# Attention with two key chunks per value group, transposed sums divided on query partitions, one value buffer and a folded value bias

## What is computed

```
q = layernorm(x) @ Wq.T + bq       # 512 queries per sequence
k = ctx @ Wk.T + bk                # 1601 keys per sequence, from ctx_1024
v = ctx @ Wv.T + bv
16 heads of depth 16
layers 0, 3: attn = softmax(q k^T / 4);  layer 2: attn = sigmoid(q k^T / 4), and no biases
x = x + (attn @ v) @ Wo.T + bo
```

## Time and profile before

| what | value |
|---|---|
| time, median of 3 runs | 3313.81 us (3311.67 to 3315.25) |
| time of the profiled execution | 3315.56 us |
| its span in the profile | 3313.7 us |
| granted PE clock, mean | 0.953 of full |
| PE busy | 2999.2 us, 91% |
| DVE busy | 1761.3 us, 53% |
| ACT busy | 1611.1 us, 49% |
| phase 0 (softmax), about | 0 to 893 us |
| phase 4 (sigmoid), about | 1568 to 2165 us |
| phase 6 (softmax), about | 2369 to 3220 us |

### The profile page before, as it was taken

One profiled execution on the slowest core, in us unless ns is written; L12 is line 12 of the kernel. 1 busy time (PEld: TensorE's weight loads), 2 busy tenths in 40 slices (PEclk: granted clock), 3 DMA queues, 4 the chain that ended last, 5 costly groups with the idle time before them and its releaser, 6 DMA issues.

```text
span 3313.7 us, 42625 instructions
## 1 busy us (share of the span) xinstructions
PE 2999.2 (91%) x16108; PEld 1521.6 (46%) x16108; DVE 1761.3 (53%) x4116; ACT 1611.1 (49%) x2747; POOL 382.8 (12%) x357
## 2 busy tenths in 40 slices
PE   5899999999799889997899999979889999999987
PEld 2234343343377658887332333257533433434333
DVE  3877776778275553332211110046477777777834
ACT  1465665656500112111577777922226656566662
POOL 3000100000110102223100010022301010000000
PEclk7999999999899999998999999989889999999996
DMA  6323224221110001000834432120243233232100
GB/s 159 83 59 77 62 51 89 54 47 24 48 34 26 1 13 45 1 1 20 198 77 105 100 86 61 24 78 1 58 104 64 66 76 62 66 76 47 24 1 30
DMA packets 119187, 190.36 MB, mean 57 GB/s; under 512 B 15900, under 2 KB 82628, under 8 KB 115912
## 3 DMA queue, kind: packets, MB, share of 16 engines
q1 hardware_dynamic: 118984, 187.65, 24.4%
HBM read 133.59 MB, written 53.63 MB: 56 GB/s over the span
## 4 chain that ended last, share of the span: by engine, by line
PE 74%; DVE 11%; ACT 6%; issue 6%; DMA 2%; SPq 1%; POOL 1%; POOLq 0%; ACTq 0%; DVEq 0%
PE psum L189 58%; PE psum L613 15%; DVE mpart L761 4%; ACT probs L665 3%; DVE rest L734 1%; ACT kp L715 1%; PE psum L274 1%; DMA qst<-q_parts_dram 1%; DVE rest L732 1%; DVE vt L752 1%; SPq L886 0%; DVE stats L301 0%; DVE x L1196 0%; ACT kp L709 0%; DMA kst<-k_parts_dram 0%
## 5 line engine op out<-in xcount | busy, mean ns | idle before, releaser
L665 ACT ACTIVATE probs<-psum 128x512 f32<-128x512 f32 (+3 forms) x2080 | 1270.8, 685 | 461.3 <-PE psum L189 459.0
L761 DVE TENSOR_REDUCE mpart<-psum 128x1 f32<-128x400 f32 (+1 forms) x2048 | 1033.4, 566 | 163.3 <-PE psum L189 161.9
L189 PE MATMUL psum<-qst,kst 115*128 115x512 bf16 (+3 forms) x2496 | 848.0, 383 | 29.3 <-ACT probs L665 20.4
L189 PE MATMUL psum<-kst,qst 112*128 112x400 bf16 (+1 forms) x2048 | 692.3, 343 | 60.7 <-DMA qst<-q_parts_dram 28.9
L613 PE MATMUL psum<-probs,vt 128*17 128x512 f32 (+1 forms) x4992 | 657.2, 598 | 33.0 <-ACT probs L665 32.7
L189 PEld LDWEIGHTS psum<-kst,qst 112*128 112x128 bf16 x2048 | 202.0, 99 | 585.2 <-DVE mpart L761 306.6
L189 PEld LDWEIGHTS psum<-qst,kst 115*128 115x128 bf16 (+3 forms) x2496 | 231.4, 100 | 428.6 <-issue 183.5
L613 PEld LDWEIGHTS psum<-probs,vt 128*17 128x17 f32 (+1 forms) x4992 | 83.1, 95 | 260.7 <-issue 167.5
L189 PE MATMUL psum<-ctxT,wk 128*128 128x512 f32 (+1 forms) x384 | 152.7, 528 | 24.5 <-DMA ctxT<-in_ctxT 21.7
L189 PE MATMUL psum<-wv,ctxT 128*128 128x256 f32 (+1 forms) x624 | 160.6, 404 | 8.5 <-ACT hT L288 4.8
L189 PE MATMUL psum<-masked_hi,w_hi 128*128 128x256 f32 x512 | 153.4, 300 | 7.9 <-DVE masked_lo L1803 7.9
(11 more groups left out here) (273 smaller groups left out, 3246.3 us busy)
## 6 DMA issues: line engine op xcount, KB each, us to landing
kst<-k_parts_dram SPq DMA_DIRECT2D x96, 600.4 KB, 8.9
k_parts_dram<-kp SPq DMA_DIRECT2D x24, 1200.8 KB, 4.4
q_parts_dram<-qp SPq DMA_DIRECT2D x168, 128.0 KB
qst<-q_parts_dram SPq DMA_DIRECT2D x48, 448.0 KB, 11.2
ctxT<-in_ctxT SPq DMA_DIRECT2D x36, 512.0 KB, 4.9
kst<-k_parts_dram SPq DMA_DIRECT2D x48, 200.1 KB, 10.4
stage<-in_L_ffn_W SPq DMA_DIRECT2D x16, 256.0 KB, 4.1
x<-in_x SPq DMA_DIRECT2D x4, 512.0 KB, 8.4
```

The lines of the kernel that those rows point to most:

```text
L189: last = e.matmul(dst, lhsT, rhs, start=i == 0, stop=i == len(pairs) - 1)
L665: e.activation(self.probs[n % slots][0:kn, :, :], c.psum[0:kn, k:k + self.wide, :], ACT.Exp if softmax else ACT.Sigmoid, scale=DH ** -0.5) ...
L761: e.tensor_reduce(self.mpart[:, row, i:i + 1], c.bank(k)[:, 0:MAX_BLOCKS[i][1]], AX.X, ALU.max).then_inc(c.drained(k), 1)
```

## The change

- `attend_steps`: `pv` now takes two key chunks in one step (8 float32 matmuls in a row, 16 records, in place of 4 and 8) behind the third head's scores of every second chunk. Chunk 12 stays alone at the unit's end, behind its scores. `PROBS` goes from 10 to 16 buffers.
- `den`, `div`, `sel_den`, `rsmall` and POOL's copy go. `turn_acc` transposes `accs` by four PE transposes, so that queries lie on partitions; DVE takes the reciprocals and multiplies 128x256 elements into `crow`. Twice per sequence `turn_ctx` turns `crow` back by four transposes, and ACT copies them to `cT`.
- In the softmax phases `wo` is dense and `proj` sums over 2 groups in place of 4. The sigmoid phase keeps its form.
- The value bias is not added to the values: `fold` computes bv @ Wo.T once a phase and adds it to `bo` (the softmax weights sum to one).
- In the softmax phases ACT evicts the values, no longer DVE. There is one `vt` buffer, so the seven `values` steps of the next sequence are put behind the `pv` steps of the fourth unit that free their places.
- Two idle slots stand between `max_close` and `max_turn`; the context load moves from 3.87 to 4.25; `proj` moves to 0.55.

```diff
-LAG = 1
-PROBS = 10
+PROBS = 16
...
-        self.vt = [c.sbuf(sc, "vt", [P, len(KEY_CHUNKS), HEADS, VW]) for _ in range(2)]
+        self.vt = c.sbuf(sc, "vt", [P, len(KEY_CHUNKS), HEADS, VW])
...
                 steps.append(("scores", f, u, kc, h))
-                if kc >= LAG and h == BEHIND:
-                    steps.append(("pv", f, u, kc - LAG))
-        return steps + [("pv", f, u, kc) for kc in range(len(KEY_CHUNKS) - LAG, len(KEY_CHUNKS))]
+                if kc >= 2 and kc % 2 == 0 and h == BEHIND:
+                    steps.append(("pv", f, u, kc - 2))
+        return steps + [("pv", f, u, LAST_KC)]
...
-            ("max_close", f, u), ("max_turn", f, u)]
+            ("max_close", f, u), ("idle",), ("idle",), ("max_turn", f, u)]
...
-                put(self.value_steps(b + 1), first + 2.5, first + 3.85, misc)
+                for i, step in enumerate(self.value_steps(b + 1)):
+                    at = first + 3 + (2 * i + 3.2) / len(KEY_CHUNKS)
+                    put([step], at, at, misc)
...
+            if softmax:
+                put([("turn_ctx", f, b, t0) for t0 in (0, 2)], first + GROUPS + 0.3, first + GROUPS + 0.5, misc)
+            put([("proj", f, b, t0) for t0 in (0, 2)], first + GROUPS + 0.55, first + GROUPS + 0.81, misc)
...
-                put([("den", f, u), ("div", f, u)], u + 1.06, u + 1.41, misc)
+                put([("turn_acc", f, u)], u + 1.1, u + 1.1, misc)
...
-                k, v = c.at(("scores", f, u, kc, GROUP - self.wide))
+                k, v = c.at(("scores", f, u, chunks[-1], GROUP - self.wide))
                 e.wait_ge(c.drained(k), v)
-                for h in range(GROUP):
...
+                for kc in chunks:
+                    kn = KEY_CHUNKS[kc][1]
+                    for h in range(GROUP):
...
                 t.then_inc(c.sem("pv_done"), 1)
...
+            elif kind == "fold":
+                e.wait_ge(c.sem("bv_spread"), c.nth[step])
+                mm(e, bank[:, 0:DM], [(self.accs[:, q * P:(q + 1) * P], self.wo[:, q, :]) for q in range(KC)]).then_inc(c.filled(k), 1)
+            elif kind == "turn_acc":
+                e.wait_ge(c.sem("evacuated"), c.nth["evacuate", f, step[2]])
                 for qt in range(SEQ // P):
-                    t = mm(e, bank[:, qt * GROUP:(qt + 1) * GROUP], [(self.accs[:, qt * P:(qt + 1) * P], c.sel_den[:, :])])
+                    at = slice(qt * P, (qt + 1) * P)
+                    t = e.transpose(bank[:, at], self.accs[:, at], c.ident[:, :])
                 t.then_inc(c.filled(k), 1)
...
+            elif kind == "values" and softmax:
+                k, v = c.at(step)
+                src, dst = self.values_of(step)
+                self.wait_values(e, step)
+                e.wait_ge(c.filled(k), v)
+                e.activation(dst, src, ACT.Copy).then_inc(c.drained(k), 1)
...
+                src = c.bank(k).rearrange("p (t h r) -> p t h r", t=4, r=32)
+                e.wait_ge(c.filled(k), v)
+                a = c.dve.count(e.reciprocal(self.rden[:, :, :], src[:, :, :, DH]))
+                e.wait_ge(c.dve.sem, a)
+                dst = self.crow[:, :, 4 * g * DH:4 * (g + 1) * DH].rearrange("p t (h d) -> p t h d", d=DH)
+                e.tensor_tensor(dst, src[:, :, :, 0:DH], self.rden[:, :, :].unsqueeze(3).to_broadcast([P, 4, GROUP, DH]),
+                                ALU.mult).then_inc(c.drained(k), 1)
```

More of the change, by code:

```diff
@@ L452, in plan @@
         self.order = in_order(placed)
-        one_bank = ("keys", "query", "values", "proj", "den", "div", "max", "max_turn", "n_turn", "scores")
+        one_bank = ("keys", "query", "values", "proj", "fold", "turn_acc", "turn_ctx", "max", "max_turn", "n_turn", "scores")
         n = 0
@@ L532, in tensor @@
             kind = step[0]
-            if kind in ("keys", "query", "values", "proj", "den", "div", "max", "max_turn"):
+            if kind in ("keys", "query", "values", "proj", "fold", "turn_acc", "turn_ctx", "max", "max_turn"):
                 k, v = c.at(step)
@@ L595, in tensor @@
             elif kind == "pv":
-                _, _, u, kc = step
+                _, _, u, first = step
                 b, g = divmod(u, GROUPS)
-                k0, kn = KEY_CHUNKS[kc]
-                if kc == 0:
-                    if g == 0:
-                        k, v = c.at(("values", f, b, LAST_KC))
-                        e.wait_ge(c.drained(k), v)
+                chunks = range(first, min(first + 2, len(KEY_CHUNKS)))
+                if first == 0:
                     if u == 0:
@@ L606, in tensor @@
                         e.wait_ge(c.sem("evacuated"), c.nth["evacuate", f, u - 1])
-                k, v = c.at(("scores", f, u, kc, GROUP - self.wide))
+                if g == 0:
+                    k, v = c.at(("values", f, b, first))
+                    e.wait_ge(c.drained(k), v)
+                k, v = c.at(("scores", f, u, chunks[-1], GROUP - self.wide))
                 e.wait_ge(c.drained(k), v)
-                for h in range(GROUP):
-                    src = ("scores", f, u, kc, h - h % self.wide)
-                    p = self.probs[self.exp_n[src] % len(self.probs)]
-                    t = e.matmul(c.bank(self.acc)[32 * h:32 * h + VW, :], self.vt[b % 2][0:kn, kc, GROUP * g + h, :],
-                                 p[0:kn, h % self.wide, :], start=kc == 0, stop=kc == LAST_KC, tile_position=(0, 32 * h))
@@ L615, in tensor @@
-                t.then_inc(c.sem("pv_done"), 1)
-            elif kind == "den":
-                u = step[2]
-                e.wait_ge(c.sem("sel_made"), 1)
-                e.wait_ge(c.sem("evacuated"), c.nth["evacuate", f, u])
+                for kc in chunks:
+                    kn = KEY_CHUNKS[kc][1]
+                    for h in range(GROUP):
+                        src = ("scores", f, u, kc, h - h % self.wide)
+                        p = self.probs[self.exp_n[src] % len(self.probs)]
+                        t = e.matmul(c.bank(self.acc)[32 * h:32 * h + VW, :], self.vt[0:kn, kc, GROUP * g + h, :],
+                                     p[0:kn, h % self.wide, :], start=kc == 0, stop=kc == LAST_KC, tile_position=(0, 32 * h))
@@ L622, in tensor @@
                 t.then_inc(c.filled(k), 1)
-            elif kind == "div":
-                u = step[2]
-                e.wait_ge(c.sem("rden_made"), c.nth["den", f, u])
-                for qt in range(SEQ // P):
-                    of = self.rden[:, qt * GROUP:(qt + 1) * GROUP, :].rearrange("p j r -> p (j r)")
-                    t = mm(e, bank[:, qt * P:(qt + 1) * P], [(of, c.ident[:, :])])
+            elif kind == "turn_ctx":
+                _, _, b, t0 = step
+                k0, v0 = c.at(("turn_acc", f, 4 * b + 3))
+                e.wait_ge(c.drained(k0), v0)
+                for j in range(2):
+                    for q in range(KC):
+                        at = (KC * j + q) * P
+                        t = e.transpose(bank[:, at:at + P], self.crow[:, t0 + j, q * P:(q + 1) * P], c.ident[:, :])
@@ L631, in tensor @@
                 _, _, b, t0 = step
-                if t0 == 0:
-                    e.wait_ge(*self.context_made(4 * b + 3))
+                if softmax:
+                    k0, v0 = c.at(("turn_ctx", f, b, t0))
+                    e.wait_ge(c.drained(k0), v0)
+                elif t0 == 0:
+                    e.wait_ge(c.sem("evacuated"), c.nth["evacuate", f, 4 * b + 3])
+                left = self.cT if softmax else self.ctxn
                 for j in range(2):
                     q0 = (t0 + j) * P
-                    t = mm(e, bank[:, j * DM:(j + 1) * DM], [(self.ctxn[:, g, q0:q0 + P], self.wo[:, g, :])
-                                                             for g in range(GROUPS)])
+                    t = mm(e, bank[:, j * DM:(j + 1) * DM], [(left[:, g, q0:q0 + P], self.wo[:, g, :])
+                                                             for g in range(left.shape[1])])
                 t.then_inc(c.filled(k), 1)
@@ L682, in scalar, with values_of, wait_values @@
                 norm.scalar(e, step)
+    def values_of(self, step):
+        _, _, b, i = step
+        chunks = KEY_CHUNKS[i:i + 2]
+        m, kn = len(chunks), chunks[0][1]
+        src = self.c.bank(self.c.at(step)[0])[0:kn, 0:m * DM].rearrange("p (n h d) -> p n h d", n=m, d=DH)
+        return src, self.vt[0:kn, i:i + m, :, 0:DH]
+    def wait_values(self, e, step):
+        _, _, b, i = step
+        if b == i == 0:
+            e.wait_ge(self.c.sem("values_ones"), self.past + 1)
+        if b:
+            e.wait_ge(*self.pv_done(GROUPS * b - 1, i))
     def split_of(self, step):
```

122 lines of the change are left out of this document (56 added, 66 removed).

## The result

| | before | change |
|---|---|---|
| median of 20 runs each | 3313.2 us (3307.1 to 3319.2) | 3319.9 us (3310.2 to 3325.9) |
| ratio to before, 95% interval | | 1.0017 (1.0009 to 1.0025) |
| span of the profiled execution | 3313.7 us | 3319.5 us |
| granted PE clock, mean | 0.953 | 0.948 |

What follows compares the result with a forecast made beforehand. PE at 91% was taken as the bound, with DVE's own sequence setting the pace as much in full softmax batches. Two softmax phases at -26 and sigmoid +18.5 gave -33.5, so 3280 us on the median's scale, range 3235 to 3325.

Steps and rivals of the forecast that it cites:

- rival 2: Sigmoid and softmax phases: the pair outlasts the three-bank rings and starves ACT and DVE; total +24, 3338 us; chance 0.15.
- the full batch at +3: Sigmoid phase, full batches: uncovered pairs +5, keys or queries +2, seams gained -4; +3 each, three batches +9.
- The bare sigmoid unit: Sigmoid units with little beside them: pair period 4.46 in place of 3.9, +2.7 a unit, three units +8.
- Softmax, a full batch -7.0: Full batch of four softmax units: sum of pairs, division, proj, values and max turn, -7.0 us each.
- Pairs: Full softmax batch: DVE's forced idle grows +0.60 a pair, 24 pairs, a fifth filled by other work: +11.5 us.
- values and slots, counted at -11.7: Full softmax batch: values moved to ACT net -6.7 us, the wait ahead of max turn covered, -5.
- den, div and proj, counted at -6.8: Full softmax batch, DVE's side: den and div -3.4 us, proj with half the records -3.4.
- Units 12 to 14: End of each softmax phase: two bare units at 39.1 for 39.8, -1.4 us together, and unit 12 -1.5.
- Unit 15: Last softmax unit, no maxima, ACT's: pairs +2.5 us less 1.5 for den and div, +1.
- tail: End of a softmax phase: half of proj and POOL's copy go, turn_ctx and an ACT copy come; -4 us.
- Prelude: Start of a softmax phase: seven value evictions leave DVE while it reduces unit 0's maxima; -3 us.
- rival 3: All pairs of pv: weight loads lie open between the chunks, 0.2 us at each of 288; +58, 3338 us; chance 0.05.

Runs made afterwards that it cites:

- sig_single: The changed kernel with pv taking one key chunk again in the sigmoid phase, pairs kept in the softmax phases: 3276.3 us, ratio 0.9871.
- sig_later: The changed kernel, pairs everywhere, but the sigmoid phase's pair stands one step later, behind the next chunk's first pair of heads: 3282.8 us, ratio 0.9896.
- probs10: The changed kernel with one key chunk per pv in all phases and 10 probs buffers in place of 16: 3247.3 us, ratio 0.9795.
- mix: The changed kernel with one key chunk per pv in the softmax phases and sigmoid pairs one step later: 3252.4 us, ratio 0.9803.
- all_single: The changed kernel with one key chunk per pv in all three phases, the rest of the change kept: 3244.7 us, ratio 0.9782.
- light readers: The changed kernel with sigmoids and maxima reading half their columns and exp rescaled: 3145.8 us with single chunks, 3128.7 us with pairs.

## Why the prediction was wrong

It forecast faster by 33.5 us and the profiled spans differ by +5.8. The mechanism, readers that run dry over a pair, was named, in the forecast for the sigmoid phase and in rival 2 for all; terms were mis-sized, the full sigmoid batch above all, and in the softmax batches the bound was misread. The 39 us between them are 20 in the sixteen sigmoid units, 11 in phase 0 and 8 in phase 6 with its prelude.

- **Sigmoid, +36.9 for +18.5: the step that failed is the full batch at +3.** Measured against sig_single, the pairs cost 13.2, 8.8 and 9.9 us in the three full stretches (units 0 to 3, 4 to 7, 8 to 11), all above even the +0 to +8 of the range. I had charged the 9 of 24 pairs with no other matmul beside them and let values and proj gain the seam where they fill PE. But a step of keys or queries writes no score either, and stands right behind a pair. PE then writes no score for 1.84 + 1.82 us. The change, at such a place:

```profile
1795.96 1.91 PE L630 MATMUL psum<-probs,vt 128*17 128x512 f32 x16 [0.40 <-ACT probs L683]
1797.80 1.99 PE L187 MATMUL psum<-ctxT,wk 128*128 128x512 f32 x4
1799.62 1.46 PE L187 MATMUL psum<-qst,kst 112*128 112x512 bf16 x6
1799.82 0.60 ACT L762 ACTIVATE kp<-psum 128x512 bf16<-128x512 f32 x1 [2.18 <-PE psum L187]
...
1802.77 0.60 PE L187 MATMUL psum<-qst,kst 112*128 112x512 bf16 x2 [1.69 <-ACT probs L683]
1803.68 3.54 PE L630 MATMUL psum<-probs,vt 128*17 128x512 f32 x16 [0.30 <-ACT probs L683]
1807.15 1.04 PE L187 MATMUL psum<-qst,kst 112*128 112x512 bf16 x4
```

  ACT idles 2.18, PE then waits 1.69 for ACT, and the next pair takes 3.47 (1803.68 to 1807.15) in place of 1.84, at the low clock. That is the unexpected part, below. Waits of PE for ACT of over 1.2 us number 13 in these sixteen units, and 5 in the kernel before and in sig_single alike: the step of keys starves ACT without a pair too, and the pair in front makes it frequent. Other work beside a pair was counted as cover; it lengthens the gap.
- **The bare sigmoid unit**: forecast 29.5, measured 30.1 and 30.7. The period was right, 4.53 for 4.46. The sum had five pairs paying where a unit has six, which is part of the rest.
- **Softmax, a full batch -7.0**: measured -7.1 and -4.7 in phase 0 (-7.2 and -6.6 in phase 6). That the sum came out for units 4 to 7 is luck, for its parts did not hold, and two errors cancelled. Pairs: +11.5 counted, +2.6 measured in the batch of units 4 to 7. All else: -18.5 counted, -9.7 measured. Of that, values and slots, counted at -11.7, gave +0.8; den, div and proj, counted at -6.8 for DVE, gave -10.5, which is PE's own count of 6.4 + 3.4. **The step that failed is the reading that in the full batches DVE's sequence sets the pace as much as PE does**; it is the root of both errors. DVE's 17.9 us of waits were close to the forced minimum of 13, and I took that for a bound; but the waits grew to 30.3 when DVE was relieved, with no gain.
- **Units 12 to 14**: -2.9 forecast, +1.5 measured in both softmax phases. This is 4.4 of the 11.3 us missing in phase 0, more than any other term (prelude 3.7, units 8 to 11 2.3, unit 15 0.8); the full batch that the misreading concerns came out near its sum. The step that failed here is the count of a bare unit as DVE's throughout, 39.1 us: it took 41.5, and the last 9 us of unit 14 have no maxima and are ACT's, as shown.
- **Unit 15** (+1; +1.8 and +1.0) and the **tail** (-4; -3.9 and -2.9): near. **Prelude** (-3): +0.7, but this term is not measured. Kernels whose prelude is the same have their first score up to 5.6 us apart: 110.0 to 111.4 with pairs in the softmax phases (the change, sig_later, sig_single), 105.8 to 107.1 with single chunks (probs10, mix, all_single), although no pv stands ahead of it. Why is open.
- **Seam and weight loads**: 1.84 for the pair came out to the hundredth, and rival 3 with its open loads fell. The Trainium skill ("TensorE: Matmul & The Clock Gate", Part 3, The mechanism) has weight loads overlap running matmuls only in another row group, though the same section also lets a load into a background weight buffer run ahead; the pair rows above, sixteen matmul records in 1.84 us, speak against the first for these tiles.
- **Rivals**: nearest came rival 2, the pair starves its readers. Its -15 for a softmax phase was met (-14.7, -16.4), but by luck, for in a full batch it had pairs at +14.4 where +2.6 to +3.8 was measured. Its +54 for the sigmoid phase was 17 too much, and its 3338 stood 18 above the result; I gave it 0.15. The test that I used against it, "half the sigmoid stretches hold keys, values or proj", was the wrong way round. The Trainium skill's warning beside it ("Trainium Kernel Development and Optimization", Best Practices), that tiling does not speed up the evacuation of PSUM, fits the light readers: 75 us of loss became 17 us of gain by lighter evacuation alone.

## What to carry to other kernels

Before work on PE is put together into longer groups, compare the longest stretch in which PE writes nothing for a reader with what the ring holds for it (at most banks times the reader's time), and count in that stretch every other step that stands next to it. A seam saved is about 0.2 us here; a starved reader costs 0.4 to 0.6 us a time (here 0.44 a pair in the last softmax unit, 0.62 in a bare sigmoid unit) and, where both wait for each other, the clock. To find out which of two close engines is the bound, see whether the waits of one grow when its own work is taken away; near-equal busy sums don't tell.
